# Attention on one core: the value matmuls of four heads issued in one step instead of two heads at a time

## What is computed

```python
scores = jnp.einsum('bhqd,bhkd->bhqk', q, k) * hs ** (-0.5)
p = jax.nn.softplus(scores)
p = p * p
p = p * causal
attn = p / (jnp.sum(p, axis=-1, keepdims=True) + 1e-09)
out = jnp.einsum('bhqk,bhkd->bhqd', attn, v)
```

## Time and profile before

| | us |
|---|---|
| median of 3 runs (lowest, highest) | 1729.88 (1729.46, 1731.93) |
| the profiled execution's own time | 1730.23 |
| its span, first to last instruction | 1728.2 |
| busy in the span: PE, DVE, ACT, POOL | 1650.6, 1192.8, 849.5, 601.8 |
| TensorE's granted clock, mean over the span | 0.99 of full speed |
| line 1366, value matmuls, busy (2048 records in the page's row) | 286.8 |
| line 1404, softplus, busy (288) | 280.7 |
| line 1420, squares on DVE, busy (176) | 262.9 |
| line 1483, squares on POOL, busy (112) | 221.4 |

### The profile page before, as it was taken

The page is one execution under the profiler, slowest core; times in us unless marked ns, Lnnn a source line. Parts: engine busy times, 40 slices in busy tenths (PEclk is TensorE's granted clock), DMA queues, the critical chain, the costliest instruction groups (busy, mean ns, idle before and its releaser), DMA issues. The chain is left out here.

```text
span 1728.2 us, 28920 instructions
## 1 busy us (share of the span) xinstructions
PE 1650.6 (96%) x11188; PEld 1149.8 (67%) x11188; DVE 1192.8 (69%) x2418; ACT 849.5 (49%) x1324; POOL 601.8 (35%) x478
## 2 busy tenths in 40 slices
PE   8999888999999999989999999998999999899999
PEld 7888774333333333368888777786777777677787
DVE  5455897666566656656556888876877777778876
ACT  4332686555555555643332232227888887522220
POOL 0002116555555555550004422211465555411111
PEclk9999999999999999999999999998999999999999
DMA  5000266636355463300001100002232323200000
GB/s 169 2 1 13 74 195 136 85 50 94 55 82 67 70 78 57 42 2 13 1 0 37 32 1 1 1 1 64 93 105 99 99 99 100 98 13 13 25 25 25
DMA packets 57016, 95.79 MB, mean 55 GB/s; under 512 B 7760, under 2 KB 29488, under 8 KB 56880
## 3 DMA queue, kind: packets, MB, share of 16 engines
q1 hardware_dynamic: 55920, 93.35, 24.5%
q10 hardware_dynamic: 960, 0.59, 0.1%
HBM read 76.88 MB, written 17.04 MB: 54 GB/s over the span
## 5 line engine op out<-in xcount | busy, mean ns | idle before, releaser
L1404 ACT ACTIVATE att_weights<-ps 128x1024 f32<-128x1024 f32 (+1 forms) x288 | 280.7, 976 | 193.2 <-PE ps L1345 106.0
L1420 DVE TENSOR_TENSOR att_weights<-att_weights 128x1024 f32<-128x1024 f32 (+1 forms) x176 | 262.9, 1504 | 86.8 <-ACT att_weights L1404 86.8
L1366 PE MATMUL ps<-att_weights,att_v_ones 64*32 64x64 f32 (+5 forms) x2048 | 286.8, 398 | 13.9 <-DVE v L1441 13.9
L927 DVE SCALAR_TENSOR_TENSOR X<-ps,moe_gsel,X 128x256 f32<-128x256 f32 x512 | 246.1, 483 | 72.3 <-PE ps L48 50.1
L1483 POOL TENSOR_TENSOR att_weights<-att_weights 128x1024 f32<-128x1024 f32 x112 | 221.4, 1979 | 202.7 <-ACT att_weights L1404 202.0
L48 PE MATMUL ps<-w_experts_hi,moe_xh 128*128 128x512 f32 x512 | 204.1, 399 | 0.0
L48 PE MATMUL ps<-w_experts_hi,moe_xl 128*128 128x512 f32 x512 | 203.2, 397 | 0.0
L48 PE MATMUL ps<-w_experts_lo,moe_xh 128*128 128x512 f32 x512 | 201.5, 393 | 0.0
L1366 PEld LDWEIGHTS ps<-att_weights,att_v_ones 128*32 128x32 f32 (+1 forms) x2048 | 81.8, 108 | 132.4 <-issue 83.6
L424 ACT ACTIVATE ffn_gates<-ps,ffn_gate_bias 128x512 f32<-128x512 f32 x72 | 49.5, 688 | 148.2 <-PE ps L48 126.6
L48 PEld LDWEIGHTS ps<-w_experts_hi,moe_xh 128*128 128x128 f32 x512 | 96.1, 188 | 24.3
(11 more groups left out here) (281 smaller groups left out, 3742.3 us busy)
## 6 DMA issues: line engine op xcount, KB each, us to landing
ssm_lb<-decays SPq DMA_DIRECT2D x32, 512.0 KB, 4.7
ssm_rise<-decays SPq DMA_DIRECT2D x28, 512.0 KB, 3.9
qk_parts<-qkv_part SPq DMA_DIRECT2D x32, 384.0 KB, 2.8
q_stack<-qk_parts SPq DMA_DIRECT2D x64, 128.0 KB, 4.7
k_stack<-qk_parts SPq DMA_DIRECT2D x64, 128.0 KB, 8.7
att_q_stack<-qk_parts SPq DMA_DIRECT2D x64, 128.0 KB, 4.8
att_k_stack<-qk_parts SPq DMA_DIRECT2D x64, 128.0 KB, 8.3
out<-X SPq DMA_DIRECT2D x7, 512.0 KB, 3.0
```

What stands on the lines that cost most here:

```text
L927: dve.scalar_tensor_tensor(out=x, in0=ring[:, e // 2, (e % 2) * C:(e % 2 + 1) * C], scalar=gsel[:, s, j, e:e + 1], in1=x, op0=ALU.mult, op ...
L1366: ins = pe.matmul(O(qb)[h * 2 * HD:(h + 1) * 2 * HD, q0:q0 + w], values, Wt[rows, u % WU, t, c:c + w], start=kj == 0 and part == FULL, sto ...
L1404: act.activation(Wt[:, u % WU, 0:n], scores(u)[:, 0:n], ACT.Softplus).then_inc(plus_done, 1)
L1420: dve.tensor_tensor(wt, wt, wt, ALU.mult).then_inc(sq_dve, 1)
```

## The change

The values of a step's two units are no longer issued one unit at a time. `value_step` replaces `value_unit`: it waits for the squares of both units and then issues the products of all four heads, key tile by key tile. PE's order becomes, for each step: the scores of the two units that are 7 on from the step's own, then the step's values, then the transposes that are due. An UPPER step, with one unit, keeps its order. The assignment of squares to engines is written as a table (`engine_of`) with the same content; a third entry for ACT is declared and not used. AHEAD, the slots, the lags and the other engines' orders stay.

```diff
-    on_pool = lambda u: u % 5 in (1, 3)
-    pool_squares = [sum(on_pool(x) for x in range(u)) for u in range(NU + 1)]
-    dve_squares = [u - pool_squares[u] for u in range(NU + 1)]
+    BY_DVE, BY_POOL, BY_ACT = range(3)
+    engine_of = [BY_POOL if u % 5 in (1, 3) else BY_DVE for u in range(NU)]
+    squares = [[sum(engine_of[x] == e for x in range(u)) for u in range(NU + 1)] for e in range(3)]
...
-            def value_unit(i, u):
-                m = step_of[u]
+            def value_step(i, m):
                 s, (qb, last, products) = m // PS, pass_steps[m % PS]
-                if u % PU == 0:
+                base = s * PU
+                if m % PS == 0:
                     pe.wait_ge(v_copied, 2 * (2 * i + s + 1))
-                if products[0][1:3] == (0, u % PU) and products[0][-1] != UPPER:
+                if products[0][1] == 0 and products[0][-1] != UPPER:
                     pe.wait_ge(o_done, (i * 2 + s) * BLOCKS + qb + 1)
...
-                if on_pool(u):
-                    pe.wait_ge(sq_pool, i * pool_squares[NU] + pool_squares[u + 1])
-                else:
-                    pe.wait_ge(sq_dve, i * dve_squares[NU] + dve_squares[u + 1])
+                for u in range(base + products[0][2], base + last + 1):
+                    pe.wait_ge(squared[engine_of[u]], i * squares[engine_of[u]][NU] + squares[engine_of[u]][u + 1])
                 for h, kj, unit, t, c, q, w, part in products:
-                    if unit == u % PU:
...
-                if last == u % PU:
-                    ins.then_inc(pv_done, 1)
+                ins.then_inc(pv_done, 1)
...
             def body(i, first=False, last=False):
-                for u in range(NU):
-                    if not (last and u + AHEAD >= NU):
-                        score_unit(i, u + AHEAD)
-                    value_unit(i, u)
-                    outputs_at(u, BLOCK_UNITS, NU, TURN_LAG, i, first, turn_output)
+                for m in range(NS):
+                    begin, end = step_end[m - 1] + 1 if m else 0, step_end[m] + 1
+                    for u in range(begin, end):
+                        if not (last and u + AHEAD >= NU):
+                            score_unit(i, u + AHEAD)
+                    value_step(i, m)
+                    for u in range(begin, end):
+                        outputs_at(u, BLOCK_UNITS, NU, TURN_LAG, i, first, turn_output)
```

More of the change, by code:

```diff
@@ L1320, in attention_phase @@
         s_done, plus_done, pv_done = sem("s_done"), sem("plus_done"), sem("pv_done")
-        sq_pool, sq_dve = sem("sq_pool"), sem("sq_dve")
+        sq_dve, sq_pool, sq_act = squared = sem("sq_dve"), sem("sq_pool"), sem("sq_act")
         oT_done, o_turned, den_done, rec_done, o_done = (sem(n) for n in ("oT_done", "o_turned", "den_done", "rec_done", "o_done"))
@@ L1356, in value_unit @@
                         pe.matmul(O(qb), ident16[:, :], neg[:, 0:1].broadcast_to([P, BANK]), start=True, stop=False)
-                if on_pool(u):
-                    pe.wait_ge(sq_pool, i * pool_squares[NU] + pool_squares[u + 1])
-                else:
-                    pe.wait_ge(sq_dve, i * dve_squares[NU] + dve_squares[u + 1])
+                for u in range(base + products[0][2], base + last + 1):
+                    pe.wait_ge(squared[engine_of[u]], i * squares[engine_of[u]][NU] + squares[engine_of[u]][u + 1])
                 for h, kj, unit, t, c, q, w, part in products:
-                    if unit == u % PU:
[L1363 to L1367, removed]
-                if last == u % PU:
-                    ins.then_inc(pv_done, 1)
+                    q0 = q - qb * BANK
+                    rows = slice(h % 2 * HALF, (h % 2 + 1) * HALF) if part == UPPER else slice(0, P)
+                    values = va_up[rows, s, kj, h // 2] if part == UPPER and h % 2 else va[rows, s, kj, h]
+                    ins = pe.matmul(O(qb)[h * 2 * HD:(h + 1) * 2 * HD, q0:q0 + w], values,
+                                    Wt[rows, (base + unit) % WU, t, c:c + w], start=kj == 0 and part == FULL, stop=part == UPPER and kj == (qb + 1) * GT - 1)
+                ins.then_inc(pv_done, 1)
             def turn_output(n, i, k):
@@ L1445, in body @@
                 for u in range(NU):
-                    if not on_pool(u):
+                    if engine_of[u] == BY_DVE:
                         square(i, u)
@@ L1479, in body @@
                 for u in range(NU):
-                    if on_pool(u):
+                    if engine_of[u] == BY_POOL:
                         pool.wait_ge(plus_done, SU + i * NU + u + 1)
```

## The result

The changed kernel takes 1657.97 us (median of 4 runs, 1654.93 to 1660.01) against 1730.91 us for the kernel before on the same chip: a ratio of 0.958, 95% interval 0.956 to 0.960, 73 us saved. The prediction was 1666 us with a range of 1644 to 1700.

What follows compares the result with a forecast made beforehand. PE was taken to bound the kernel at 30.05 us a pass; afterwards squares, at 24.63 plus waits of 0.53 and 0.5, give 25.7. That saves 64 us of 1729.9: 1666 us, range 1644 to 1700.

Steps and rivals of the forecast that it cites:

- The bound before: Attention stage of the old kernel: PE sets the pace, at 30.05 us a pass.
- Four heads wide: PE's value matmuls: a step's two units take 0.98 us instead of 1.96, saving 7.8 us a pass.
- third rival: PE's values: the four heads don't run together, a step takes 1.84 us, total 1714 us; chance 0.03.
- Scores and the joint wait at nothing: PE's paired scores (at worst 4 us a pass) and its wait for both units' squares: each taken as zero.
- The squares late next, by exclusion: Attention stage after the change: mutually exclusive DVE and POOL squares set the pace, 25.7 us a pass.
- DVE's busy time: DVE per pass: squares of DVE and POOL plus outputs, 25.92 us, less 1.29 hidden, 24.63.
- the wait for ACT: DVE's waits in the saturated start of the stage, carried over as 0.53 us a pass.
- the estimate for the transposes: DVE at line 1432: waiting for PE's transposes adds an estimated 0.5 us a pass.
- the signs listed: Profile signs of being right, among them PE busy well under 0.9, bodies 51.4 us apart, PE waiting for squares.
- DVE's wait for the transposes: First rival, DVE at line 1432: the wait stays near 3.1 us a block, total 1703 us; chance 0.10.
- squares would not bind: Second rival, attention stage: PE's 22.2 us a pass sets the pace, total 1610 us; chance 0.04.
- fourth rival: PE loses its clock through gathered idle time; at half, 32.0 us a pass, total 1761 us; chance 0.03.

Runs made afterwards that it cites:

- two-wide run: The changed kernel with the FULL and REST products of heads 2 and 3 sent to the columns of heads 0 and 1, their outputs left out: 1699.08 us.
- half squares: The changed kernel with every square, on DVE and POOL alike, covering only half the columns: 1592.19 us, ratio 0.919.

## Why the prediction held, point by point

**The bound before: right.** PE set the pace; squares without POOL moved the old kernel by 7.5 us and the new one by 51.

**Four heads wide: right, to the hundredth.** The step was put at 0.98 us and takes 0.99. The evidence was the last body's end, where four matmuls shared a span, and the two-wide run shows its other side: 1.84, the figure given for the third rival. That rival's total, 1714 us, was 15 too high: it left out that the waits for a bank's division would shrink too, 10 us, and that the scores gain by standing two units in a row.

**Scores and the joint wait at nothing: right for the wait, off for the scores.** The joint wait alone measured nothing. The scores, put at zero or a loss, gained 0.09 us a step, and PE's own pass without waits came out at 20.9 us rather than 21.3. Neither shows in the time, since PE no longer sets the pace.

**The squares late next, by exclusion: right.** The pass was put at 25.7 us and measured 25.13; 16 x 0.57 = 9 us is nearly all of the difference between the 64 us forecast and the 73.5 of the stage. The total came closer than that because 3.4 us were lost outside the stage, where the prediction had no change; that is luck. Of the terms, DVE's busy time was put at 24.63. Cut at the stack loads, the six bodies 299.70 to 601.23 us are (the view by windows, first, second and fourth body, and the sums):

```profile
299.70:350.02 50.32, 44.56 (x574) 20.35 (x578) 48.29 (x39) 33.29 (x36) 38.86 (x18) 0.94 0.62 85
350.02:399.12 49.10, 41.93 (x574) 19.81 (x578) 48.84 (x39) 33.52 (x37) 40.38 (x18) 1.00 0.65 87
...
447.51:500.37 52.86, 45.36 (x574) 21.16 (x577) 49.72 (x39) 33.62 (x37) 42.80 (x19) 0.90 0.61 81
...
sum 301.53, PE 261.37 PEld 122.06 DVE 292.25 ACT 201.18 POOL 239.72; mean PE 43.56 PEld 20.34 DVE 48.71 ACT 33.53 POOL 39.95
```

292.25 / 12 = 24.35 us busy and 0.77 idle a pass, against 24.63 and 1.03. The largest miss is the wait for ACT: taken over at 0.53 a pass from the saturated start, it was 9.3 - 7.05 = 2.25 us in all behind the first square, 0.14 a pass. DVE's busy time was 0.28 too high, and the estimate for the transposes, 0.5, was too low, 10.8 / 16 = 0.68; the misses cancel in part. (The upper bound of the pass, 27.9, is 28.0 by its own terms.) A POOL square at its whole mean length of 1.98 us would have made it 27.6 a pass; the 1.71 from the saturated rows came nearer. The Trainium skill (SBUF — State Buffer, section on who interferes with whom) calls the port pair of DVE and POOL an exclusive lock: with that the run without POOL agrees, whose squares on DVE take 1.21 us where there had been 2.08, but a whole instruction is more than these rows charge. Of the signs listed, PE's busy share came to 0.87, and PE's waiting for squares hardly showed, 0.4 us; it waited for the copy and the division.

**The rivals.** DVE's wait for the transposes did not stay, 10.8 us after 96.1; it was still a near thing, as the run with TURN_LAG 5 shows. That squares would not bind is refuted by the runs without POOL and with half squares; PE's own pass, named there at 22.2, is 20.9. PE did lose its clock in places, which the prediction gave as the sign of its fourth rival: 0.90 in the slowest body, 52.86 us, and 1.00 in one of 49.10, of the two levels 1.2 and 2.4 GHz. At 0.96 over the 120.20 us above, about 8% of the time was at the lower level, far from the 41% of PE's work that the rival needed, so the kernel did not become slower. But the loss did not all fall into the room that PE had, as was foreseen. Here are two blocks of the changed kernel in which PE waited equally long, 2.75 us, for the copy ahead of the transposes, each with DVE's wait for the next transposes (the timelines of PE and DVE, then the view by windows from the end of PE's wait):

```profile
365.68 0.66 PE L1371 MATMUL ps<-ident,att_oT 128*128 128x128 f32 x4 [2.75 <-DVE att_oT L1425]
373.69 0.17 DVE L1431 TENSOR_SCALAR att_den<-ps 128x16 f32<-128x16 f32 x1
...
414.77 0.93 PE L1371 MATMUL ps<-ident,att_oT 128*128 128x128 f32 x4 [2.75 <-DVE att_oT L1425]
422.92 0.17 DVE L1431 TENSOR_SCALAR att_den<-ps 128x16 f32<-128x16 f32 x1 [1.23 <-PE ps L1371]
...
365.68:369.68 4.00, 2.75 (x48) 1.69 (x48) 3.96 (x6) 2.79 (x3) 3.92 (x3) 1.00 0.22 27
414.77:418.77 4.00, 4.00 (x45) 2.27 (x46) 3.96 (x6) 1.23 (x2) 3.92 (x3) 0.57 0.15 20
```

At full clock DVE then waits for nothing; at 0.57 it waits 1.23 us. Over the stage, 13 of the 32 blocks had a granted clock under 1.00 in the 10 us ahead of line 1431, and eight of these waited 0.94 to 1.94 us, 10.1 us in all; of the other 19 only the last one waited, 0.75 us. An estimate of what the lower clock cost is therefore 10 us of the stage's 402.6, nearly all of DVE's wait for the transposes; it rests on what goes together in one trace, and no run changed the clock alone. In the slowest body two such waits, 1.94 and 0.94 us, make up most of the 3.14 us for which DVE was idle, against 0.26 in the body at 1.00.

## What to carry to other kernels

Matmuls with a stationary operand of 32 columns ran four abreast where they stood next to one another in PE's queue, and two abreast where the scores, on the full array, stood between them; look at the end of a loop, where the interleaved work has run out, for what the engine can do. When a bound is lifted by a quarter, add up the next engine's chain from the stretch in which it was already saturated: here the first two passes gave the pass after the change within 2.3%. Where two engines exclude each other, count what each instruction adds to the common chain rather than busy shares, and give the work to the engine that adds least.

## What was not expected

That POOL's help with the squares cost time: its 14 squares a body cost the changed kernel 51 us, since one adds 1.71 us to the chain and the same square on DVE 1.13. By these terms it would be 112 x 0.58 = 65 us; part of that was given back, since some of DVE's outputs had run beside POOL's squares (0.66 of 1.29 us in the stretch that the prediction sums up). The terms of the prediction had both numbers side by side, and I did not draw the conclusion until the run was planned. And that one unit of lag for the transposes costs 22 us: DVE's order makes it wait there with all squares behind it, and the clock falls as well.
